# Seven node steps in a row between the first loads and the first tile of the message stage

## The chip, the cores and the metric

The kernel runs on one core of a Trainium2 chip. The metric is the device time of one execution in microseconds (us), the median over several executions. Engines are named PE (TensorE, matmuls and transposes), DVE (VectorE), ACT (ScalarE), POOL (GpSimd) and SP (SyncE, which here only issues DMAs and waits).

## What is computed

A graph network with two message-passing layers over 50000 nodes of 256 features and 12500 edges sorted by destination. Each layer adds its result to the node rows and normalises them:

```python
x = _layernorm(x + _L0_gnn_ref(x, edge_index, L0_gnn_W, L0_gnn_attn, L0_gnn_W_out), axis=-1)
x = _layernorm(x + _L1_gnn_ref(x, edge_attr_64, edge_index, ...), axis=-1)
```

The first layer is attention over the edges (scores, softmax over the edges of one destination, weighted sum, product with W_out). The second layer has the same shape with queries, keys and values, adds edge attributes, and mixes its result with a skip product under a sigmoid gate:

```python
x_r = m @ Wskip.T + bskip
beta = jax.nn.sigmoid(jnp.concatenate([out, x_r, out - x_r], axis=-1) @ Wbeta.T)
out = beta * x_r + (1.0 - beta) * out
return out @ W_m2n.T
```

A node that no edge ends in has out = 0 in both layers, so its row is a normalisation, one product with a folded matrix, a gated add and a second normalisation. Rows that edges end in are computed apart, by edge, and scattered over the first result at the end.

## The kernel before

There are two kinds of work. **Node steps** (class Nodes) take all 50000 rows, 256 rows (two tiles of 128) at a time, as if no edge ended in any: 196 steps, 205 with the drain of their pipeline. **Edge tiles** are 100 tiles of 125 edges that pass through stages in turn: score, first softmax (soft1), gather, message, second softmax (soft2), output. A softmax stage is one serial chain over all tiles. Edge tiles of one stage write rows to DRAM which the next stage reads.

One hand-written list, the plan, holds (part, step) entries. Each engine walks the same plan from first to last and issues what that part does on it at that step, so that on each engine the order of instructions is the plan's, and an instruction that waits holds up all that stands behind it on its engine. The function blend spreads two lists evenly through each other. NODE_SHARE says how many node entries are blended into the start (74), soft1 (10), gather (66), message (45) and soft2 (10).

A node entry s works on several steps of the pipeline at once, by `live(s, lag, total)`. On SP it issues the load of step s + 2 (L635), and then the store of step s - 9 (L651). X has 12 slots, and the load must wait for the slot's earlier store to have landed. That is the store of step s - 10, which the node entry just ahead has issued:

```python
n = s + self.AHEAD
at_least(sp, self.moved[n % U], 32 * (n // U))
load(n)
```

On DVE a node entry takes the statistics of row block s (L763, waits for its load), the gated add of s - 5 (L770), the aggregate (L778) and, at every second entry, the normalisation of s - 2 (L784; at the others one small operation L757 for ACT, which then normalises). On PE it issues four transposes (L734) and four matmuls with the folded matrix (L744). On POOL it computes 1/sqrt of the variances with L666 and L671; DVE and ACT of the next entry wait for it. ACT copies, squares and scales; the scaled rows are what the store waits for.

A gather entry's PE part is two transposes (L1210) and two matmuls (L1217) after a scan on DVE (L1243). Each tile's row block is loaded from rows, added to, and stored again (L1186). A message entry t, from -6 to 102, loads on SP the row block of tile t + 5 (L1337) and for every second tile a line of picks (L1340), and issues on POOL the indirect gather of source rows for tile t + 5 (L1307). Entry -6 clears a buffer (DVE L1426) and loads edge attributes (L1347). At entry -5 three things stand in front of the first loads: POOL waits until all stores of the gather stage have landed, then gathers 100 tail rows (L1304); SP waits for those, writes them to DRAM (L1334), and waits for that write. DVE takes statistics of tile t + 3 (L1440, L1453), compares picks of tile t + 2 (L1459) and normalises tile t + 1 (L1467). From entry 0 on PE transposes tile t (L1367, L1369), and one entry later it computes keys, values and queries (L1382, L1383, L1387). POOL's L1315 and L1318 compute 1/sqrt for two tiles together.

Of the kernel before, what the change touches and what calls it, by code (L numbers as in the profile page):

```python
# [71 lines left out]
def blend(lists):  # L72

    spread = [((2 * k + 1) / (2 * len(x)), n, entry) for n, x in enumerate(lists) for k, entry in enumerate(x)]
    return [(n, entry) for _, n, entry in sorted(spread, key=lambda e: e[:2])]
# [1588 lines left out]
def main_pass(nc, c, io, out):  # L1664

    with ExitStack() as ctx:
# [21 lines left out]
        output = Output(nc, c, ctx, out, masks, nodes, message, soft2)  # L1688
        parts = (nodes, score, finder, soft1, gather, message, soft2, output, made, masks, positions)
        plan = order_of(parts, NODE_SHARE)  # L1690

        with nc.Block() as block:
# [28 lines left out]
                    emits[n](s)  # L1721


NODE_SHARE = (74, 10, 66, 45, 10)
NODE_NORMED = ["A" if 74 <= s < 84 or s >= 186 else "AD"[s % 2] if s >= 84 else "D" for s in range(NSTEPS)]
NODE_SCALED = ["AD"[s % 2] if s < 66 else "A" for s in range(NSTEPS)]

# [1 line left out]
def order_of(parts, share):  # L1729


    nodes, score, finder, soft1, gather, message, soft2, output, made, masks, positions = range(11)
    entries = [[(n, s) for s in range(p.FIRST, p.LAST)] for n, p in enumerate(parts)]
    at = share[0]
    plan = start_of(entries[score], entries[finder], entries[nodes][0:at], entries[made], entries[masks], entries[positions])
    for count, group in zip(share[1:], ((soft1,), (gather,), (message,), (soft2,))):
        lists = [entries[nodes][at:at + count]] + [entries[n] for n in group]
        at += count
        plan += [entry for _, entry in blend(lists)]
    assert at == len(entries[nodes])  # L1740
    return plan + entries[output]
# [8 lines left out]
def start_of(score, finder, nodes, made, masks, positions):  # L1750


    before = {}
    for at, part in ((MADE_AT, made), (MASKS_AT, masks), (POSITIONS_AT, positions)):
        for t, entry in zip(at, part):
            before.setdefault(t, []).append(entry)
    steps = [e for e in score]
    plan = []
    for at, tiles in ((Score.FIRST, NODES_FROM), (NODES_FROM, FINDER_FROM), (FINDER_FROM, Score.LAST)):
        part = steps[at - Score.FIRST:tiles - Score.FIRST]  # L1760
        share = round(len(nodes) * len(part) / (Score.LAST - NODES_FROM)) if tiles < Score.LAST else len(nodes)
        now = [] if at < NODES_FROM else nodes[:share]
        nodes = nodes[len(now):]
        lists = [now, part] + ([finder] if at == FINDER_FROM else [])
        for n, entry in blend(lists):
            if n == 1:
                plan += before.pop(entry[1], [])
            plan.append(entry)
    assert not nodes and not before
    return plan  # L1770
# [92 lines left out]
```

How the kernel before makes its waits and increments, by code:

```python
def at_least(eng, sem, value):  # L50
    if value > 0:
        eng.wait_ge(sem, value)
# [118 lines left out]
        @block.sync  # L172
# [16 lines left out]
                sp.dma_start(w.w_n2m, io["L1_gnn_W_n2m"]).then_inc(c.ldd, 16)  # L189
                for k in range(2):
                    sp.dma_start(w.w_edge[:, k, :], io["L1_gnn_W_edge"]).then_inc(c.ldd, 16)
                for k in range(2):
                    sp.dma_start(c.wo[:, k, :], io["L0_gnn_W_out"][k * P:(k + 1) * P, :]).then_inc(c.ldd, 16)
                sp.wait_ge(dve_done, 4)
                sp.dma_start(w.previ[1:TILES, :], rows[0:TILES - 1, EDGES - 1:EDGES]).then_inc(c.edge_loads, 16)
                sp.dma_start(w.nexti[0:TILES - 1, :], rows[1:TILES, 0:1]).then_inc(c.edge_loads, 16)
# [3 lines left out]
        @block.scalar  # L200
        def _(act):
            with nc.allow_non_contiguous_dma(reason="one bias column"):
                for out, name in ((w.bq_xr[:, 0:DM], "bq"), (w.bq_xr[:, DM:2 * DM], "bskip"), (w.b_kv[:, 0:DM], "bk"), (w.b_kv[:, DM:2 * DM], "bv")):
                    act.dma_start(out, io["L1_gnn_" + name].rearrange("(a d) -> a d", a=1).to_broadcast([P, DM])).then_inc(c.ldd, 16)
                act.dma_start(w.bs_cols[:, 0:1], io["L1_gnn_bskip"].rearrange("(d a) -> d a", a=1)).then_inc(c.ldd, 16)
            act.wait_ge(turned, 1)
            for k, out in enumerate((c.src_col, c.dst_col)):
                act.activation(out[:, :], c.psum[:, 0, k * 256:k * 256 + TILES], ACT.Copy).then_inc(turned, 1)
```

## Time and profile before

| | us |
|---|---|
| median of 3 executions | 1315.22 |
| lowest and highest | 1313.17, 1316.82 |
| profiled execution, whole | 1313.72 |
| its span, first to last instruction | 1311.9 |
| PE busy | 1170.9 (89%) |
| DVE busy | 1050.2 (80%) |
| ACT busy | 841.8 (64%) |
| POOL busy | 836.8 (64%) |

In the trace the first softmax lies at about 390 to 440 us, the gather stage at 440 to 727, the message stage at 727 to 1075. Busy time is the time in which an engine executes; a row of a timeline gives start and duration of merged instructions, how many, and in square brackets how long the engine was idle before them and what ended the wait. A row of SP gives the issue of a DMA, not its transfer. LDWEIGHTS (PEld) runs beside PE's matmuls.

### The profile page before, as it was taken

How to read it: one execution, taken by the hardware profiler on the slowest of the kernel's cores; microseconds unless marked ns; L12 is line 12 of the kernel's file. 1: busy time of each engine (PE TensorE's matmuls, PEld its weight loads, DVE VectorE, ACT ScalarE, POOL GpSimd, SP SyncE). 2: the span in 40 equal slices, each digit the busy share in tenths (PEclk: the TensorE clock that was granted, in tenths of full speed). 3: DMA queues.
4: the chain of work that ended last, by engine and by line, in shares of the span. 5: the costliest groups of instructions: out<-in, count | busy, mean ns of one | idle time of the engine just before them, and what ended most of it. 6: DMA issues, size and time to landing. Idle time of an engine off the chain costs nothing. (4 is left out here: it accounts for less than half of the span.)

```text
span 1311.9 us, 28292 instructions
## 1 busy us (share of the span) xinstructions
PE 1170.9 (89%) x6986; PEld 1022.4 (78%) x6986; DVE 1050.2 (80%) x3776; ACT 841.8 (64%) x2783; POOL 836.8 (64%) x1044
## 2 busy tenths in 40 slices
PE   3999999999996789989999599999999993999991
PEld 3888998989985577778777498999999982788880
DVE  3667777777779798899888599999999977788881
ACT  1566666666667756656666466666666675799992
POOL 4888888888853445445453566667767732377775
PEclk9999999999998999999999799999999997999996
DMA  5768988888863478878787777777767732556641
GB/s 155 237 207 268 280 258 265 257 282 268 260 223 121 145 230 237 244 239 258 225 251 213 230 218 216 213 215 233 218 213 218 218 105 86 163 184 191 191 157 56
DMA packets 208938, 277.05 MB, mean 211 GB/s; under 512 B 40060, under 2 KB 140563, under 8 KB 208777
## 3 DMA queue, kind: packets, MB, share of 16 engines
q1 hardware_dynamic: 188793, 224.13, 55.5%
q0 software_dynamic: 19264, 50.85, 13.4%
q8 instruction: 60, 0.98, 0.3%
q14 instruction: 101, 0.83, 0.2%
q10 hardware_dynamic: 720, 0.26, 0.1%
HBM read 159.73 MB, written 117.12 MB: 211 GB/s over the span
## 5 line engine op out<-in xcount | busy, mean ns | idle before, releaser
L744 PE MATMUL banks<-m_ext,node_XT 128*128 128x257 f32 x1568 | 377.1, 383 | 0.0
L744 PEld LDWEIGHTS banks<-m_ext,node_XT 128*128 128x128 f32 x1568 | 286.0, 192 | 32.8
L671 POOL TENSOR_TENSOR node_r<-node_vv,half 128x4 f32<-128x4 f32 (+1 forms) x202 | 211.9, 1049 | 17.2 <-POOL node_vv L666 0.5
L702 ACT ACTIVATE node_XT<-banks 128x512 f32<-128x512 f32 x196 | 117.1, 597 | 153.1 <-PE banks L734 150.1
L770 DVE SCALAR_TENSOR_TENSOR node_X<-banks,node_be,node_X 128x256 f32<-128x256 f32 x392 | 169.2, 473 | 56.3 <-ACT node_be L696 56.0
L666 POOL TENSOR_SCALAR node_vv<-node_mv 128x4 f32<-128x4 f32 (+1 forms) x202 | 54.9, 272 | 200.6 <-DVE node_mv L778 180.5
L763 DVE BATCH_NORM_STATS2 node_st<-node_X 128x6 f32<-128x256 f32 x392 | 145.7, 413 | 20.6 <-DMA node_X<-in_x 19.4
L709 ACT ACTIVATE node_sq<-node_X 128x256 f32<-128x256 f32 x392 | 157.5, 406 | 0.0
L683 ACT ACTIVATE node_X<-node_X,node_r 128x256 f32<-128x256 f32 x326 | 146.0, 496 | 16.3 <-POOL node_r L671 16.2
L734 PE MATMUL banks<-ident,node_X 128*128 128x128 f32 x784 | 122.4, 279 | 31.9 <-DVE node_X L784 16.8
L824 POOL DMA_INDIRECT ring<-in_x,src_col x100 | 110.7, 1107 | 36.4 <-POOLq L171 13.7
L734 PEld LDWEIGHTS banks<-ident,node_X 128*128 128x128 f32 x784 | 95.6, 149 | 44.9 <-issue 19.7
L1307 POOL DMA_INDIRECT ring<-rows,src_pos x100 | 107.3, 1073 | 22.8 <-issue 20.3
L784 DVE TENSOR_SCALAR node_X<-node_X,node_mv,node_r 128x256 f32<-128x256 f32 x250 | 91.1, 406 | 34.0 <-POOL node_r L671 34.0
L824 POOL DMA_INDIRECT ring<-in_x,dst_col x100 | 98.2, 982 | 31.5 <-issue 29.0
L857 PE MATMUL banks<-wh,ST 128*128 128x260 f32 x400 | 105.3, 386 | 1.1
L870 ACT ACTIVATE ST<-banks 128x512 f32<-128x512 f32 x100 | 59.3, 593 | 73.0 <-PE banks L847 71.4
L1538 POOL DMA_INDIRECT out<-store,last_col x90 | 89.1, 990 | 26.3 <-issue 20.0
L1382 PE MATMUL banks<-w_kv,ST 128*128 128x256 f32 x400 | 104.9, 385 | 0.3 <-DVE store L1430 0.3
L1580 PE MATMUL banks<-m_ext,AT 128*128 128x257 f32 x400 | 104.3, 383 | 0.0
L1217 PE MATMUL banks<-wo,AT 128*128 128x256 f32 x400 | 103.0, 380 | 0.2 <-DVE ring L1234 0.2
L1243 DVE TENSOR_TENSOR_SCAN AT<-MB,AT,banks 128x128 f32<-128x128 f32 x198 | 83.9, 465 | 18.7 <-PE banks L1210 13.4
(267 smaller groups left out, 2674.6 us busy)
## 6 DMA issues: line engine op xcount, KB each, us to landing
node_X<-in_x SPq DMA_DIRECT2D x196, 256.0 KB, 3.8
out<-node_X SPq DMA_DIRECT2D x196, 256.0 KB, 3.3
ring<-rows SPq DMA_DIRECT2D x210, 128.0 KB, 4.2
rows<-ring SPq DMA_DIRECT2D x100, 256.0 KB, 4.4
rows<-ring SPq DMA_DIRECT2D x200, 128.0 KB, 3.5
MB<-keeps SPq DMA_DIRECT2D x40, 320.0 KB, 5.2
store<-rows SPq DMA_DIRECT2D x90, 128.0 KB, 4.1
MB<-picks SPq DMA_DIRECT2D x50, 128.0 KB, 3.9
```

What stands on the lines that cost most here:

```text
L671: pool.tensor_tensor(r[:, s % 4, NT * lo:NT * hi], v, self.c.half[:, NT * lo:NT * hi], ALU.pow).then_inc(self.roots, 1)
L683: last = eng.activation(row, row, ACT.Identity, scale=rz)
L702: act.activation(self.XT[:, n % 2, :], c.psum[:, 4, 0:NT * D], ACT.Copy, bias=1.0).then_inc(self.xt_ready, 1)
L709: last = act.activation(self.sq[:, k, :], X[:, n % U, k, :], ACT.Square, scale=1.0 / D ** 0.5, accum_out=self.mv[:, s % 4, 1, k, 1:2])
L734: last = pe.transpose(ps[:, 4, k * D + h * P:k * D + (h + 1) * P], self.X[:, n % U, k, h * P:(h + 1) * P], c.ident[:, :])
L744: last = pe.matmul(ps[:, NT * o + k, 0:D + 1], self.XT[:, o, k * D + h * P:k * D + (h + 1) * P], c.m_ext[:, h, :], start=(h == 0), stop=(h ...
L763: last = dve.bn_stats(st[:, s % 2, k, :], X[:, s % U, k, :])
L770: last = dve.scalar_tensor_tensor(out=X[:, n % U, k, :], in0=ps[:, b + k, 0:D], scalar=self.be[:, n % 4, k:k + 1], in1=X[:, n % U, k, :], ...
L824: pool.indirect_dma_start(out=c.ring[:, n % R, side, :], out_offset=None, in_=self.x, in_offset=bass.IndirectOffsetOnAxis(ap=col[:, n:n + ...
L857: pe.matmul(ps[:, 6, 0:HP], c.ST[:, o, h * P:(h + 1) * P], c.wh[:, h, :], start=(h == 0), stop=(h == 1))
L1307: pool.indirect_dma_start(out=c.ring[:, n % R, 1, :], out_offset=None, in_=c.rows, in_offset=bass.IndirectOffsetOnAxis(ap=c.src_pos[:, n:n ...
L1382: pe.matmul(ps[:, 6, 0:2 * DM], c.ST[:, o, h * P:(h + 1) * P], c.w_kv[:, h, :], start=(h == 0), stop=(h == 1))
```

## The change

Two node entries move from the gather stage to the message stage (NODE_SHARE 66 and 45 become 64 and 47). The message stage's first three entries (-6, -5, -4), which issue the loads and gathers of tiles 0 and 1, come first without nodes between them. Then seven node entries follow in a row, and only then the other 106 message entries blended with the other 40 node entries. The rest of the program is unchanged.

```diff
-NODE_SHARE = (74, 10, 66, 45, 10)
+NODE_SHARE = (74, 10, 64, 47, 10)
+NODES_AT_MESSAGES = 7
+MESSAGES_AFTER = 3
...
     for count, group in zip(share[1:], ((soft1,), (gather,), (message,), (soft2,))):
-        lists = [entries[nodes][at:at + count]] + [entries[n] for n in group]
+        now, others = entries[nodes][at:at + count], [entries[n] for n in group]
         at += count
+        if group == (message,):
+            plan += others[0][:MESSAGES_AFTER] + now[:NODES_AT_MESSAGES]
+            now, others = now[NODES_AT_MESSAGES:], [others[0][MESSAGES_AFTER:]]
+        lists = [now] + others
         plan += [entry for _, entry in blend(lists)]
```

On SP at the start of the message stage, before the change (L1347 is entry -6, each pair L635 and L651 a node entry, L1334 the write of the tail rows, L1337 a tile's row block):

```order
L1347 DMA MSG<-in_edge_attr 125x4x64
L635 DMA node_X<-in_x 128x512
L651 DMA out<-node_X 128x512
L1334 DMA rows<-AT 100x256
L1337 DMA ring<-rows 128x256
L1340 DMA MB<-picks 128x256
L1337 DMA ring<-rows 128x256 x2
L1340 DMA MB<-picks 128x256
L635 DMA node_X<-in_x 128x512
L651 DMA out<-node_X 128x512
L1337 DMA ring<-rows 128x256
L1347 DMA MSG<-in_edge_attr 125x4x64
```

and with the change:

```order
L1347 DMA MSG<-in_edge_attr 125x4x64
L1334 DMA rows<-AT 100x256
L1337 DMA ring<-rows 128x256
L1340 DMA MB<-picks 128x256
L1337 DMA ring<-rows 128x256
L635 DMA node_X<-in_x 128x512
L651 DMA out<-node_X 128x512
L635 DMA node_X<-in_x 128x512
L651 DMA out<-node_X 128x512
...
L635 DMA node_X<-in_x 128x512
L651 DMA out<-node_X 128x512
L1337 DMA ring<-rows 128x256
```

The load of tile 2 was the third L1337, directly behind those of tiles 0 and 1; now seven node entries (the first two and the last are shown, four are like them) stand between.

On DVE from the buffer's clearing at entry -6 on, before the change (L763 to L784 are node entries, the first L1440 is entry -3):

```order
L1426 MEMSET MSG 128x512
L757 SCALAR_TENSOR_TENSOR node_nb<-node_mv,node_r 128x2
L763 BN_STATS node_st<-node_X 128x6 x2
L770 SCALAR_TENSOR_TENSOR node_X<-banks,node_be,node_X 128x256 x2
L778 BN_AGGR node_mv<-node_st 128x2 x2
L1440 BN_STATS message_st<-ring 128x6 x2
L1453 BN_AGGR message_mv<-message_st 128x2 x2
L763 BN_STATS node_st<-node_X 128x6 x2
L770 SCALAR_TENSOR_TENSOR node_X<-banks,node_be,node_X 128x256 x2
L778 BN_AGGR node_mv<-node_st 128x2 x2
L784 TENSOR_SCALAR node_X<-node_X,node_mv,node_r 128x256 x2
L1440 BN_STATS message_st<-ring 128x6 x2
```

and with the change, where the rows left out are five more node entries:

```order
L1426 MEMSET MSG 128x512
L757 SCALAR_TENSOR_TENSOR node_nb<-node_mv,node_r 128x2
L763 BN_STATS node_st<-node_X 128x6 x2
L770 SCALAR_TENSOR_TENSOR node_X<-banks,node_be,node_X 128x256 x2
L778 BN_AGGR node_mv<-node_st 128x2 x2
...
L763 BN_STATS node_st<-node_X 128x6 x2
L770 SCALAR_TENSOR_TENSOR node_X<-banks,node_be,node_X 128x256 x2
L778 BN_AGGR node_mv<-node_st 128x2 x2
L1440 BN_STATS message_st<-ring 128x6 x2
L1453 BN_AGGR message_mv<-message_st 128x2 x2
L763 BN_STATS node_st<-node_X 128x6 x2
```

One node entry stood ahead of the first statistics of a message tile (L1440), and now seven do. Up to tile 0 on PE there were three node entries, and now eight; up to tile 2 there were four, and now nine. In the gather stage each run of tiles between two node entries has one or two tiles: 23 runs of one and 42 of two before the change, 19 and 44 with it.

## Rows read from the trace of the kernel before

**Rows 1.** Busy time in stretches: us, then PE, PEld, DVE, ACT, POOL, clock, DMA share

```profile
460.00:700.00 240.00, 220.87 (x1183) 183.12 (x1182) 210.91 (x679) 147.50 (x487) 122.56 (x198) 1.00 0.81 241
760.00:1060.00 300.00, 296.90 (x1974) 272.43 (x1973) 281.32 (x1203) 188.96 (x553) 209.18 (x258) 1.00 0.73 217
```

**Rows 2.** Timeline of PE in the gather stage: start, duration, line, operation

```profile
457.32 0.60 PE L734 MATMUL banks<-ident,node_X 128*128 128x128 f32 x4
...
566.67 0.60 PE L734 MATMUL banks<-ident,node_X 128*128 128x128 f32 x4
...
569.93 0.60 PE L734 MATMUL banks<-ident,node_X 128*128 128x128 f32 x4
...
574.63 0.60 PE L734 MATMUL banks<-ident,node_X 128*128 128x128 f32 x4
...
714.94 0.60 PE L734 MATMUL banks<-ident,node_X 128*128 128x128 f32 x4
```

**Rows 3.** Timeline of PE in the middle of the message stage

```profile
863.11 0.60 PE L734 MATMUL banks<-ident,node_X 128*128 128x128 f32 x4
...
865.29 0.38 PE L1367 MATMUL banks<-ident,ring 128*128 128x128 f32 x2
```

**Rows 4.** Timeline of SP's DMA queue around the stage boundary

```profile
712.54 0.33 SPq L635 DMA_DIRECT2D node_X<-in_x  x1
...
726.82 0.33 SPq L635 DMA_DIRECT2D node_X<-in_x  x1
727.25 0.38 SPq L651 DMA_DIRECT2D out<-node_X  x1
...
732.46 0.30 SPq L1334 DMA_DIRECT2D rows<-AT  x1
735.86 0.32 SPq L1337 DMA_DIRECT2D ring<-rows  x1
...
736.71 0.90 SPq L1337 DMA_DIRECT2D ring<-rows  x2
```

**Rows 5.** Timeline of DVE around the stage boundary

```profile
715.38 0.75 DVE L763 BATCH_NORM_STATS2 node_st<-node_X 128x6 f32<-128x256 f32 x2 [0.45 <-DMA node_X<-in_x]
...
738.29 0.75 DVE L1440 BATCH_NORM_STATS2 message_st<-ring 128x6 f32<-128x256 f32 x2 [10.42 <-DMA ring<-rows]
...
739.24 0.72 DVE L763 BATCH_NORM_STATS2 node_st<-node_X 128x6 f32<-128x256 f32 x2
...
741.43 0.74 DVE L1440 BATCH_NORM_STATS2 message_st<-ring 128x6 f32<-128x256 f32 x2
...
749.32 0.75 DVE L1440 BATCH_NORM_STATS2 message_st<-ring 128x6 f32<-128x256 f32 x2 [0.90 <-DMA ring<-rows,src_pos]
...
750.44 0.82 DVE L1467 TENSOR_SCALAR ring<-ring,message_mv,message_r 128x256 f32<-128x256 f32 x2
```

**Rows 6.** Timeline of POOL around the stage boundary

```profile
728.22 1.15 POOL L1304 DMA_INDIRECT AT<-rows,tail_pos  x1 [2.43 <-issue]
...
744.10 1.20 POOL L1307 DMA_INDIRECT ring<-rows,src_pos  x1 [0.20 <-issue]
```

**Rows 7.** Timeline of PE around the first message tiles

```profile
745.37 0.38 PE L1367 MATMUL banks<-ident,ring 128*128 128x128 f32 x2
...
754.43 0.38 PE L1367 MATMUL banks<-ident,ring 128*128 128x128 f32 x2
```

**Rows 8.** Timeline of SP's DMA queue in the first softmax

```profile
397.07 0.38 SPq L651 DMA_DIRECT2D out<-node_X  x1
400.42 0.33 SPq L635 DMA_DIRECT2D node_X<-in_x  x1
...
406.34 0.34 SPq L651 DMA_DIRECT2D out<-node_X  x1
408.37 0.33 SPq L635 DMA_DIRECT2D node_X<-in_x  x1
...
429.79 0.33 SPq L635 DMA_DIRECT2D node_X<-in_x  x1
```

## Prediction

> **What bounds the kernel now.** I read the busy time by stretches first. In the middle of the message stage PE is busy 296.9 of 300 us at full clock [rows 1], so there a node step costs what it occupies PE: from its first transpose at 863.11 to the next tile's at 865.29, 2.18 us [rows 3]. In the gather stage PE is busy 92% and DVE 88% [rows 1]; neither is full, and a node step's price must come from the spacing of rows [rows 2]. Between the stages lies a gap, and I read it engine by engine on the timelines. POOL issues the tail gather at 728.22 [rows 6]; SP writes the tail rows at 732.46, waits for them, and issues the first row block at 735.86 [rows 4]; DVE idles 10.42 us until that lands, at 738.29 [rows 5]; PE transposes tile 0 at 745.37 and tile 2 at 754.43 [rows 7]. From there on PE hardly pauses. The change puts work into this gap, so the question is what the row of seven costs there and what it saves elsewhere.
>
> **What it saves in the gather stage.** Two node steps leave. From 457.32 to 714.94 there are 58 intervals between node steps on PE [rows 2]: 20 with one tile in them, 3.27 us each in the mean (569.93 less 566.67 is one of them), and 38 with two tiles, 5.06 us in the mean (most are 4.70, as 574.63 less 569.93). The stage goes from 23 short and 42 long intervals to 19 and 44, so it saves 4 x 3.27 - 2 x 5.06 = 3.0 us, or 4 x 3.27 - 2 x 4.70 = 3.7 with the usual long one. I take 3.3. The other bound is that steps, not tiles, set the pace: 257.6 us for 58 steps is 4.44 us each, and two save 8.9.
>
> **What it saves among the message tiles.** The milestone is tile 2 on PE, since PE works without a break from there. Before it stood four node steps of 45, so 41 came after; now nine of 47, so 38. Three steps at 2.18 us are 6.5 us. Against this being less stands nothing: PE is 99% busy there [rows 1]. If DVE (94% busy) took over, the price would be its step, 741.43 less 739.24, again 2.2 us [rows 5].
>
> **What the row of seven costs.** A node step's load waits on SP until the store that the step just ahead issued has landed. In a run of node steps this is a chain of its own: store, landing, load, next store. The trace shows it where the gather stage drains: four steps from 712.54 to 726.82, 3.57 us each [rows 4], and DVE waits for their loads, as at 715.38, 2.84 us after the issue at 712.54 [rows 4, 5]. PE would need 2.18, DVE 2.2. So SP's DMAs set the pace of a row of node steps, and nothing hides them.
>
> Nor can the row start inside the wait. On SP the seven stand behind the write of the tail rows and the wait for it, so the first of them issues its load at about 737.2, after the second row block (736.71 and half of its 0.90 us [rows 4]). POOL meets the first of the seven only after the tail gather at 728.22 and two tile gathers. From what was loaded already, DVE and PE can do two steps in the gap; the third needs the load of 737.2.
>
> From there, in the clock of the trace before: the seventh node load at 737.2 + 6 x 3.57 = 758.6, its store at 759.0 (0.43 later, as 727.25 after 726.82 [rows 4]), the row block of tile 2 at 759.5. Its landing and the start on DVE took 2.43 us (735.86 to 738.29 [rows 4, 5]), so DVE has it at 761.9. This load is late because it moved behind the seven; tiles 0 and 1 have lain ready since 740. DVE's entry for tile 2 also normalises tile 0, behind the statistics of tile 2. Such an entry takes 749.32 to 750.44 and 0.82 more, 1.9 us [rows 5]. Tile 0 is on PE at 763.8, 18.4 us later than at 745.37 [rows 7].
>
> The next entries: SP's eighth node step waits for the store of 759.0 until 762.2 (3.14 us, which is 3.57 less the 0.43), so the row block of tile 3 goes out at 763.0 and is there at 765.5. DVE works on it until 767.4, does a node step (2.2) until 769.6, and the entry of tile 4 (1.9), behind which tile 2 is normalised at 771.5. POOL's gather for tile 4 must wait for the inverse roots of tiles 0 and 1, about 762.5, and takes 5.2 us (744.10 to 749.32 [rows 5, 6]), which is 767.9 and not late. Tile 2 is on PE at about 771.4 instead of 754.43: 17.0 us later.
>
> **The sum.** 17.0 - 6.5 - 3.3 = +7.2 us. Against the profiled execution's 1313.72 that is 1320.9; the median of the runs shown is 1.5 higher, 1315.22, so I predict 1322.4 us, 0.55% slower. Put another way, five more steps go into a stretch that grows by 17.0 us, 3.4 us a step, and are paid back at 2.0.
>
> **A rule against the row.** The node store of 256 KB lands 3.1 to 3.4 us after its issue when a load of the same size stands right before it: 3.35 from 397.07 to 400.42, in a stretch where next to nothing else moves [rows 8]. The store issued alone at 406.34 lets the next load go at 408.37, after 2.03 us [rows 8]. In the row of seven every store follows a load by 0.43 us, so I keep 3.57 for the step. The Trainium skill (DMA: Bandwidth & Descriptors, section on the anatomy of one DMA) puts a transfer at a fixed 2.0 us, mostly waiting for the write's receipt, and its bytes at 436 GB/s; an estimate by that page is 2.6 us for a store, 3.0 a step, and a sum of about +3.9. The row with the load ahead speaks against it, the lone store for something shorter still.
>
> **The rivals.**
> - Stores land quickly because little else is moving, at 2.03 us as the lone one [rows 8]. The step is then 2.46, six intervals save 6.7, and the sum is +0.5: 1315.7. For it speaks the lone store, against it the 3.35 us in the same quiet stretch. The same page's section on latency says that lighter load on HBM shortens the fixed part, which is this rival. Chance 0.09.
> - Node steps set the gather stage's pace, 4.44 us each [rows 2]: 17.0 - 6.5 - 8.9 = +1.6, 1316.8. Against it: intervals differ by their tiles, 3.27 and 5.06. Chance 0.14.
> - The other side: the wait covers the row. If the node steps run while DVE waits its 10.42 us [rows 5], five more of them at 2.18 are 10.9, so tile 2 is late by only 0.5 us, and 0.5 - 6.5 - 3.3 = -9.3: 1305.9. It decides on SP at the wait for the tail rows: tile 2 must be late by less than 9.8 us for any gain, by less than 5.9 for one to be seen. Against it stands the order on SP and POOL, where the seven are behind that wait. Chance 0.10.
> - ACT's scaled rows come late for the stores, as in the first softmax, where five steps from 408.37 to 429.79 took 4.28 each [rows 8]. Six intervals add 4.3: 1326.7. There the softmax held up DVE and ACT; the row of seven has nothing between, but PE's clock may drop after the idle time and lengthen the chain a little. Chance 0.13.
> - That the change doesn't do what it says is ruled out by the order of the two programs.
>
> **Numbers.** The forecast keeps 0.54. About 0.3% is what a measurement of this kernel can tell from no change, 3.9 us here. Slower by more: most of 0.54 and all of 0.13, less a small part for a forecast too high by half, 0.63. Within 0.3%: the two rivals at +0.5 and +1.6 and that part, 0.26. Faster: 0.11. The range of 1314.5 to 1328.0 takes in all but the third rival and some remainder: below it reaches under +0.5, above to +4.3 on the forecast and a little more for first tiles at a lower clock.
>
> **What the changed profile would show.** On SP seven pairs of node load and store 3.5 to 3.7 us apart, with waits for the node store, and L1337 for tile 2 some 22 us after those of tiles 0 and 1. DVE waiting before L763 in the row rather than before the first L1440. Tile 0 (first L1367) 17 to 19 us later, seen from the tail gather L1304. The tail gather itself some 3.3 us earlier than 728.22, and from tile 2 to the end of the message stage 6.5 us less. I am wrong if the pairs stand 2.5 us apart, if the gather stage shrinks by 8 us, or if some pairs come before L1334.

## The result

The changed kernel takes 1318.99 us (median of 8, 1315.41 to 1321.31) against 1314.04 us for the kernel before on the same chip (median of 8, 1309.12 to 1316.82): a ratio of 1.0035, 95% interval 1.0021 to 1.0049, or 4.6 us slower by the ratio and 4.95 by the medians. The forecast was 7.2 us slower, and 1322.4 us. Its profiled execution has a span of 1315.8 us, 3.9 more than before.

Three points in time cut the trace into parts: POOL's first weighted row of the gather stage (L1175), the tail gather (L1304), and tile 2 of the message stage on PE (third L1367). The first is read from the view of one line, here of the kernel before and then of the changed one; the pair of times is that of the first and the last such instruction.

```profile
L1175 POOL TENSOR_TENSOR MSG<-store,weights x100: 608/614/617, 440.1 to 701.1; 128x256 f32<-128x256 f32 x100
```

```profile
L1175 POOL TENSOR_TENSOR MSG<-store,weights x100: 607/612/616, 438.1 to 691.7; 128x256 f32<-128x256 f32 x100
```

The tail gather on POOL's timeline of the changed kernel, which answers to the first line of [rows 6]:

```profile
717.76 1.15 POOL L1304 DMA_INDIRECT AT<-rows,tail_pos  x1 [5.83 <-issue]
```

So the gather stage took 728.2 - 440.1 = 288.1 us before and 717.8 - 438.1 = 279.7 with the change. On PE's timeline, as in [rows 7], the first three message tiles, and two of the node steps ahead of them (L744, eight matmuls, 1.90 us at full clock):

```profile
730.75 2.86 PE L744 MATMUL banks<-m_ext,node_XT 128*128 128x257 f32 x8 [2.77 <-DVE node_X L770]
...
736.00 3.14 PE L744 MATMUL banks<-m_ext,node_XT 128*128 128x257 f32 x8
...
754.83 0.69 PE L1367 MATMUL banks<-ident,ring 128*128 128x128 f32 x2 [6.95 <-DVE ring L1467]
...
759.74 0.38 PE L1367 MATMUL banks<-ident,ring 128*128 128x128 f32 x2
...
762.42 0.44 PE L1367 MATMUL banks<-ident,ring 128*128 128x128 f32 x2 [0.32 <-DVE ring L1467]
```

Tile 2 comes at 762.42, 44.7 us after the tail gather; before it was 26.2 us (754.43 less 728.22). Between them lies the row of seven. SP's queue there, as in [rows 4]:

```profile
721.28 0.28 SPq L1334 DMA_DIRECT2D rows<-AT  x1
...
724.59 0.42 SPq L1337 DMA_DIRECT2D ring<-rows  x1
725.05 0.43 SPq L635 DMA_DIRECT2D node_X<-in_x  x1
725.58 0.38 SPq L651 DMA_DIRECT2D out<-node_X  x1
729.75 0.33 SPq L635 DMA_DIRECT2D node_X<-in_x  x1
...
733.37 0.33 SPq L635 DMA_DIRECT2D node_X<-in_x  x1
...
744.55 0.33 SPq L635 DMA_DIRECT2D node_X<-in_x  x1
...
748.46 0.33 SPq L635 DMA_DIRECT2D node_X<-in_x  x1
...
749.35 0.43 SPq L1337 DMA_DIRECT2D ring<-rows  x1
```

The first node load of the row goes at 725.05, behind the tail rows and the row block of tile 1, and the seventh at 748.46: six intervals of 3.90 us in the mean. Each load but the first waits for the landing of the store just ahead, the first time from 725.58 to 729.75; by the view of SP's waits these six waits hold 18.2 us. The row block of tile 2 goes out at 749.35, 24.8 us after that of tile 1. DVE waits for node rows in the row, as it waited for the tile's row block before [rows 5]:

```profile
722.88 0.73 DVE L784 TENSOR_SCALAR node_X<-node_X,node_mv,node_r 128x256 f32<-128x256 f32 x2 [2.33 <-POOL node_r L671]
...
729.07 0.75 DVE L763 BATCH_NORM_STATS2 node_st<-node_X 128x6 f32<-128x256 f32 x2 [4.69 <-DMA node_X<-in_x]
...
739.76 0.75 DVE L763 BATCH_NORM_STATS2 node_st<-node_X 128x6 f32<-128x256 f32 x2 [1.95 <-DMA node_X<-in_x]
...
745.01 0.72 DVE L1440 BATCH_NORM_STATS2 message_st<-ring 128x6 f32<-128x256 f32 x2
...
752.92 0.76 DVE L1440 BATCH_NORM_STATS2 message_st<-ring 128x6 f32<-128x256 f32 x2 [1.66 <-issue]
```

At 722.88 it ends the second step of the row, which needs no further load; from 729.07 on it waits for the loads. Tile 0's statistics (L1440, 745.01) follow the row directly, and tile 2's at 752.92 stand between them and the normalisation of tile 0.

The lengths of the parts, for all kernels that ran. "Row" is the change's row of node entries; "last" is the last L1367. The first two and the next two lines are the same kernel twice.

| kernel (gather/message shares) | gather stage | tail gather to tile 2 | tile 2 to last | last to end | median us |
|---|---|---|---|---|---|
| before (66/45) | 288.1 | 26.2 | 316.1 | 241.3 | 1314.04 |
| before again | 288.4 | 24.8 | 316.9 | 241.9 | (one: 1314.36) |
| changed (64/47, row) | 279.7 | 44.7 | 311.7 | 241.7 | 1318.99 |
| changed again | 276.7 | 44.9 | 311.5 | 242.6 | (one: 1316.21) |
| shares alone (64/47) | 281.1 | 25.5 | 317.4 | 243.2 | 1304.87 |
| row alone (66/45) | 284.5 | 45.5 | 306.7 | 241.7 | 1323.34 |
| two in a row (64/47) | 280.2 | 27.3 | 320.3 | 242.4 | 1309.85 |
| row behind six (64/47) | 278.6 | 38.3 | 312.7 | 241.9 | 1314.01 |
| shares 58/53 | 263.4 | 25.1 | 329.4 | 244.3 | 1298.04 |
| before, 13 slots | 271.9 | 25.2 | 316.7 | 243.0 | 1297.45 |
| changed, 13 slots | 267.0 | 38.6 | 310.5 | 242.9 | 1298.67 |
| shares 58/53, 13 slots | 257.6 | 23.6 | 329.4 | 243.7 | 1295.11 |
| row behind six, 13 slots | 265.8 | 37.8 | 312.5 | 241.6 | 1299.81 |
| row behind six, 58/53, 13 slots | 255.7 | 40.4 | 322.4 | 244.8 | 1302.38 |

The medians come from four sessions, in which the kernel before stood at 1312.3 to 1314.0; ratios below are each against the runs of before in its own session. One profiled execution may lie 2 to 5 us from its kernel's median (1319.46 against 1323.34 for the row alone, 1303.28 against 1298.04 for the shares 58/53), so a part's length is good to some 2 us, and the gather stage's to 4: up to there the three kernels with 66 entries run the same program but for the last node entry, and theirs took 284.5 to 288.4 us, and the five with 64 took 276.7 to 281.1. With 13 slots the mark between the first two columns moves too. In the kernel before with 13 slots the tail gather comes 6.3 us after the last store of the gather stage (SP 704.51 to POOL 710.82), held up on POOL by the one node entry ahead of it; with the row that entry stands behind it, and it comes 3.0 us after (701.92 to 704.96). So 3.3 us of what the gather stage loses and the stretch gains between those two lines is only the mark. With 12 slots it comes 4.2 and 4.1 us after in the two kernels.

### The profile page after: what moved, and what is told of

It is laid out like the page before. It is cut to its first block and busy times, and to the rows that moved or that the text cites. A ratio compares the mean times of both kernels' runs of the same rounds, so it can differ in the third digit from the quotient of the medians.

```text
span 1315.8 us, 28292 instructions
## 1 busy us (share of the span) xinstructions
PE 1177.1 (89%) x6986; PEld 1025.7 (78%) x6986; DVE 1050.6 (80%) x3776; ACT 841.7 (64%) x2783; POOL 835.8 (64%) x1044
## 5 line engine op out<-in xcount | busy, mean ns | idle before, releaser
L744 PE MATMUL banks<-m_ext,node_XT 128*128 128x257 f32 x1568 | 381.1, 386 | 2.8 <-DVE node_X L770 2.8
L744 PEld LDWEIGHTS banks<-m_ext,node_XT 128*128 128x128 f32 x1568 | 288.6, 194 | 36.7 <-issue 3.1
L671 POOL TENSOR_TENSOR node_r<-node_vv,half 128x4 f32<-128x4 f32 (+1 forms) x202 | 211.4, 1047 | 17.3 <-ACT node_X L683 0.4
L702 ACT ACTIVATE node_XT<-banks 128x512 f32<-128x512 f32 x196 | 117.0, 597 | 143.0 <-PE banks L734 140.1
L763 DVE BATCH_NORM_STATS2 node_st<-node_X 128x6 f32<-128x256 f32 x392 | 145.9, 414 | 26.9 <-DMA node_X<-in_x 25.9
L683 ACT ACTIVATE node_X<-node_X,node_r 128x256 f32<-128x256 f32 x326 | 146.1, 496 | 21.9 <-POOL node_r L671 21.9
L734 PE MATMUL banks<-ident,node_X 128*128 128x128 f32 x784 | 123.7, 281 | 27.9 <-DVE node_X L784 13.1
L784 DVE TENSOR_SCALAR node_X<-node_X,node_mv,node_r 128x256 f32<-128x256 f32 x250 | 91.5, 408 | 42.8 <-POOL node_r L671 42.8
L870 ACT ACTIVATE ST<-banks 128x512 f32<-128x512 f32 x100 | 59.3, 593 | 70.8 <-PE banks L847 68.6
L1409 ACT ACTIVATE ST<-banks 128x512 f32<-128x512 f32 x100 | 59.3, 593 | 67.5 <-PE banks L1369 67.5
```

Of the source, the lines that this page charges most:

```text
L671: pool.tensor_tensor(r[:, s % 4, NT * lo:NT * hi], v, self.c.half[:, NT * lo:NT * hi], ALU.pow).then_inc(self.roots, 1)
L683: last = eng.activation(row, row, ACT.Identity, scale=rz)
L702: act.activation(self.XT[:, n % 2, :], c.psum[:, 4, 0:NT * D], ACT.Copy, bias=1.0).then_inc(self.xt_ready, 1)
L734: last = pe.transpose(ps[:, 4, k * D + h * P:k * D + (h + 1) * P], self.X[:, n % U, k, h * P:(h + 1) * P], c.ident[:, :])
L744: last = pe.matmul(ps[:, NT * o + k, 0:D + 1], self.XT[:, o, k * D + h * P:k * D + (h + 1) * P], c.m_ext[:, h, :], start=(h == 0), stop=(h ...
L763: last = dve.bn_stats(st[:, s % 2, k, :], X[:, s % U, k, :])
```

## The experiments

**The change in halves.** First the shares without the row.

```diff
-NODE_SHARE = (74, 10, 66, 45, 10)
+NODE_SHARE = (74, 10, 64, 47, 10)
```

> Only the shares change: two node entries go from the gather stage to the message stage (64 and 47), blended evenly in both, no row of seven. Theory A (my prediction's terms): the gather stage saves 3.3 us by the count of its short and long intervals, two more steps among message tiles cost 2 x 2.2, so +1.1 us. Theory B (from the changed kernel's trace, whose gather stage, first weighted row to tail gather, was 279.7 us instead of 288.2): fewer steps there save 8.5 us by themselves, so -4.1 us, and the gather stage of this run is also near 280.

Measured: 1304.87 us, ratio 0.9944 (0.9928 to 0.9960), 7.4 us faster. My terms fall; the gather stage of this run is 281.1 us. The two steps are worth 7 us there by this trace against that of before, and theory B holds, with more gained than its 4.1 us.

Then the row without the shares, that is the changed kernel with

```diff
-NODE_SHARE = (74, 10, 64, 47, 10)
+NODE_SHARE = (74, 10, 66, 45, 10)
```

> Only the row of seven: shares as before (66 and 45), the first three message entries, seven node entries, then the rest. Theory A: tail gather to tile 2 on PE grows by 17 to 18.5 us as in the changed kernel, and five steps fewer after tile 2 give 10.9 back: +6.1 to +7.6 us. Theory B (node steps are worth less among tiles, 1.8 us): +8.5 to +9.5 us. Theory C (the stretch between the stages costs less when it isn't preceded by a shorter gather stage): below +4.

Measured: 1323.34 us, ratio 1.0090 (1.0073 to 1.0107), 11.8 us slower. The stretch is 45.5 us, 19 to 21 longer than before, and tile 2 to last gives back 9.4 to 10.2 for five steps. That is nearest to theory B, but its time is above the bounds of all three, since the stretch grew by more than any of them had. This trace's gather stage, 284.5 us, is 3.7 shorter than the mean of the two of before with the same shares; it is the execution that lies 3.9 us below its kernel's median. The halves add up: -7.4 + 11.8 = +4.4 us, against +4.6 for both together.

**The wait for the store just issued.** With 13 slots instead of 12, the load of step s + 2 waits for the store of step s - 11, which the node entry before the last has issued. To make room, the squares that nothing reads are stored as bf16; the ACT instruction that writes them takes 408 ns in the median instead of 407.

```diff
-    U = 12
+    U = 13
...
-        self.sq = sb("sq", [P, NT, D])
+        self.sq = sb("sq", [P, NT, D], mybir.dt.bfloat16)
```

The kernel before, so changed:

> The kernel before with 13 instead of 12 slots for node rows (room for it by storing the unused squares as bf16): a node's load then waits for the store two steps back and not for the one just issued. Theory A (the store's landing paces node steps only where they stand in a row): the five steps where the gather stage drains take some 2.5 us instead of 3.57, 4 to 6 us are saved there and in the first softmax, and the gather stage's inner intervals stay at 3.3 and 4.7 to 5.1. Theory B (the landing also paces the inner gather stage): the long intervals lose their excess over 4.7 and the stage shrinks by more than 10 us.

Measured: 1297.45 us, ratio 0.9882 (0.9864 to 0.9900), 15.5 us faster. What SP waited for between 460 and 690 us (total, times, longest), in the kernel before and then with 13 slots:

```profile
SPq L635 <- DMA out<-node_X: 74.0, 47, 4.5
...
SPq L1186 <- DVE ring L1234: 5.6, 15, 0.8
```

```profile
SPq L1186 <- DVE ring L1234: 40.8, 33, 2.3
SPq L53 <- ACT node_X L683: 37.9, 32, 2.6
```

The wait of the node load for a landing store, 74.0 us over 47 times, is gone; SP now waits for what the engines have ready, scaled node rows from ACT (L683) and edge rows from DVE (L1234). The bf16 squares weren't run with 12 slots, so that they do nothing for the time rests on ACT's unchanged duration. The gather stage shrinks from 288.1 to 271.9 us, so theory B holds: the long intervals between node steps on PE (two tiles in them, 5.06 us in the mean before [rows 2]) are 4.72 us in the mean now, 38 of them in either trace. The landing of stores paced part of the inner gather stage too. This is the fact that my gather term had wrong.

The changed kernel with 13 slots:

> The changed kernel with 13 slots. Theory A (the wait of a load for the store just issued sets the pace of the row of seven): the seven node loads stand 2.2 to 2.7 us apart instead of 3.9 in the mean, the stretch from the tail gather to tile 2 shrinks by 7 to 9 us, and the change costs nothing any more against the kernel before with 13 slots (-4 to 0 us). Rival (the engines' own chain or PE's lower clock after the idle time sets the pace): the loads stay 3.3 us or more apart and the change still costs 3 us or more.

Measured: 1298.67 us, above the kernel before with 13 slots by 1.2 us by the medians and by 2.8 by the ratios (0.9903 and 0.9882 to the same runs, whose intervals overlap), where the change cost 4.6 with 12. So it costs less, but the forecast of -4 to 0 isn't shown. SP's node loads in the row:

```profile
712.23 0.43 SPq L635 DMA_DIRECT2D node_X<-in_x  x1
...
713.18 0.43 SPq L635 DMA_DIRECT2D node_X<-in_x  x1
...
717.21 0.33 SPq L635 DMA_DIRECT2D node_X<-in_x  x1
...
725.73 0.43 SPq L635 DMA_DIRECT2D node_X<-in_x  x1
727.50 0.34 SPq L651 DMA_DIRECT2D out<-node_X  x1
```

From 712.23 to 725.73 there are six intervals of 2.25 us in the mean, where they were 3.90, so the chain of store, landing and load is shown to have set the pace. The waits for landing stores aren't all gone: four of them hold 6.5 us in this row, against six and 18.2. The stretch shrinks from 44.7 to 38.6 us, by 6.1 where 7 to 9 were expected, and not to the 25.2 of the kernel without a row. On PE the node steps now follow each other like this:

```profile
721.47 0.60 PE L734 MATMUL banks<-ident,node_X 128*128 128x128 f32 x4
...
724.58 0.63 PE L734 MATMUL banks<-ident,node_X 128*128 128x128 f32 x4 [0.77 <-issue]
...
727.08 0.66 PE L734 MATMUL banks<-ident,node_X 128*128 128x128 f32 x4
...
730.24 0.63 PE L734 MATMUL banks<-ident,node_X 128*128 128x128 f32 x4 [0.77 <-issue]
```

That is 8.77 us for three steps, 2.92 us each, where PE needs 2.18 [rows 3]: with no tiles between them, PE waits in each or in every second step until rows have gone through the other engines. The fullest of them is ACT, busy for 8.02 of these 8.77 us, with PE at 7.11 and DVE at 6.50.

**Fewer in the row.** Two instead of seven, which is as many as are already loaded:

```diff
-NODES_AT_MESSAGES = 7
+NODES_AT_MESSAGES = 2
```

> The changed kernel with two node entries in a row instead of seven (shares 64 and 47 as changed). Two steps' rows are loaded before SP waits for the tail rows. Theory A (only steps beyond the two loaded ones cost the interval of 3.6 to 3.9 us): tail gather to tile 2 on PE takes 26 to 28 us instead of 44.7, and the time stands within 3 us of the kernel with only the shares changed (-7.4 against the kernel before). Rival (the first tiles suffer from anything that stands before them, by the row blocks loaded late): the stretch is 32 us or more, the time 5 us or more over the shares alone.

Measured: 1309.85 us, ratio 0.9977 (0.9961 to 0.9993), 3.0 us faster than before but over 4 slower than the shares alone by the ratios, which is between the two theories' bounds. The stretch is 27.3 us, as theory A has it; 1.8 us of the difference are there, and some 3 lie between tile 2 and the last tile (320.3 against 317.4). Some 2 of these are one node step more: 42 stand between those two tiles on PE, and 41 with the shares alone, which has one more behind the last tile (243.2 against 242.4 us to the end). From two to seven in the row the stretch grows by 17.3 us, 3.46 us a step.

**The row behind six message entries.** Five row blocks are then issued ahead of the row, and tile 0 is normalised.

```diff
-MESSAGES_AFTER = 3
+MESSAGES_AFTER = 6
```

> The row of seven moves behind six message entries instead of three: row blocks and gathers of tiles 0 to 4 are issued and tile 0 is normalised before the seven; tile 0 on PE comes right behind them. Theory A (of the 19 us, 6 or 7 intervals are the node loads' chain and some 8 us are the row block of tile 2 that comes late and the tile pipeline started anew): tail gather to tile 2 takes 36 to 38 us instead of 44.7, with 8 node steps before tile 2 instead of 9, and the time is 5 to 8 us below the changed kernel's, near that of before. Rival (the chain of node loads is all of it): no better than 2 us below the changed kernel.

Measured: 1314.01 us, ratio 1.0007 (0.9991 to 1.0024): level with before, some 3.7 us below the changed kernel by the ratios. PE's timeline:

```profile
719.87 0.66 PE L1358 MATMUL banks<-ident,MSG 128*128 128x128 f32 x2 [6.31 <-DMA MSG<-in_edge_attr]
...
731.25 1.09 PE L734 MATMUL banks<-ident,node_X 128*128 128x128 f32 x4 [6.43 <-issue]
...
749.20 0.38 PE L1367 MATMUL banks<-ident,ring 128*128 128x128 f32 x2
...
752.34 0.38 PE L1367 MATMUL banks<-ident,ring 128*128 128x128 f32 x2
...
754.87 0.44 PE L1367 MATMUL banks<-ident,ring 128*128 128x128 f32 x2 [0.17 <-DVE ring L1467]
```

Tile 0 follows the row at once and tile 1 after 3.1 us, where it was 4.9, and the stretch is 38.3 us, just above the expected 36 to 38. The time gained, 3.7 us, is less than the 5 to 8 of theory A and more than the 2 of its rival. One reason stands in the first two lines: PE first waits 6.31 us for the edge attributes, with node steps ready behind, and then 6.43 us more, since DVE takes the tiles' statistics before the row. The gap that the first steps of the row had filled is empty again.

**Both together.** The row behind six entries and 13 slots:

> The changed kernel's row of seven behind six message entries, with 13 slots: both suspected costs are taken away, the chain of node loads behind stores and the late row block of tile 2. Theory A (these two are the whole excess of the stretch): tail gather to tile 2 takes 31 to 33 us, with four more node steps before tile 2 than in the kernel before with 13 slots (25.2 us), so under 2 us a step; the time is 1294 to 1297, level with or below the 1297.5 of the kernel before with 13 slots. Rival (something else in the row costs, such as PE's lower clock or the engines' own chain): the stretch stays at 36 us or more and the time at 1298 or above.

Measured: 1299.81 us, ratio 0.9899 (0.9882 to 0.9917). Theory A falls, and its rival holds: the stretch is 37.8 us. SP's queue, PE's timeline and ACT's in the row:

```profile
729.26 0.70 SPq L635 DMA_DIRECT2D node_X<-in_x  x1
732.38 0.34 SPq L651 DMA_DIRECT2D out<-node_X  x1
732.76 0.94 SPq L635 DMA_DIRECT2D node_X<-in_x  x1
734.53 0.34 SPq L651 DMA_DIRECT2D out<-node_X  x1
```

```profile
710.25 0.66 PE L1358 MATMUL banks<-ident,MSG 128*128 128x128 f32 x2 [4.67 <-DMA MSG<-in_edge_attr]
...
719.24 1.09 PE L734 MATMUL banks<-ident,node_X 128*128 128x128 f32 x4 [4.06 <-issue]
...
722.85 0.60 PE L734 MATMUL banks<-ident,node_X 128*128 128x128 f32 x4
...
734.10 0.66 PE L734 MATMUL banks<-ident,node_X 128*128 128x128 f32 x4
```

```profile
726.62 0.60 ACT L702 ACTIVATE node_XT<-banks 128x512 f32<-128x512 f32 x1
...
729.14 0.60 ACT L702 ACTIVATE node_XT<-banks 128x512 f32<-128x512 f32 x1 [0.28 <-PE banks L734]
...
732.27 0.60 ACT L702 ACTIVATE node_XT<-banks 128x512 f32<-128x512 f32 x1
```

SP's loads and stores alternate and hardly a load waits for a store any more (0.3 us in all); the stores wait for scaled rows instead (17.0 us by the view of waits, nine times from 700 to 760 us, for ACT). PE does the last four steps from 722.85 to 734.10, 2.81 us each. And PE idles in the gap as before. So beyond the two costs there is a third, and the traces name the engine: two steps take ACT 5.65 us, from the copy (L702) at 726.62 to that at 732.27, and the 0.28 before 729.14 are all it idles in them. ACT is busy for 10.51 of the 11.25 us of the four steps, PE for 9.47 and DVE for 7.33. A node step occupies ACT for some 2.7 us, since every step's rows are scaled there and every second step's also normalised; that is more than PE's 2.18 and DVE's 2.2, the two that my prediction compared. No run moved work off ACT, so that a row would then go faster is not shown.

PE's clock isn't the reason in these steps: the granted clock is 1.00 from 722.85 to 734.10 here, and 1.00 in the three steps of the changed kernel with 13 slots shown above. In the whole stretch it was 0.81 and 0.85 in the two traces of the changed kernel and 0.74 and 0.79 in those of before, so some steps run at half the clock (L744 in 2.86 and 3.14 us above), but the row didn't lower it. That the gap can be filled only by what stands ahead of DVE's first tile is my reading of the order of the work; no run put the row there.

**How the gather stage prices a node step.** Eight entries moved instead of two, no row:

```diff
-NODE_SHARE = (74, 10, 66, 45, 10)
+NODE_SHARE = (74, 10, 58, 53, 10)
```

> The kernel before with 58 node entries blended into the gather stage and 53 into the message stage. My prediction's terms (a gather stage of intervals of 3.27 and 5.06 us: 16 short ones fewer, 8 long ones more; 2.18 us a step in the message stage): gather -11.8, message +17.4, so +5.6 us. What the shares alone showed (gather about 3 us a step, message 1.5 to 1.8): gather -24, message +13, so -9 to -13 us. If the gain of the shares alone was a matter of where the two steps stood, it doesn't grow: -7 to 0.

Measured: 1298.04 us, ratio 0.9890 (0.9866 to 0.9915), 14.4 us faster, a little beyond the 9 to 13 that the shares alone led me to expect. The gather stage is 24.7 us shorter, 3.1 us a step, and tile 2 to last 13.3 longer, 1.7 a step. The forecast from my prediction's terms, +5.6 us, has even the sign wrong. The same with 13 slots:

> The same shares, 58 and 53, with 13 slots, so that a load doesn't wait for the store just issued. Theory A (part of a node step's price in the gather stage is the landing of stores, which 13 slots take away, and the rest PE's 3.26 and 4.72 us intervals): the gather stage is 13 to 16 us shorter than with 66 steps and 13 slots, the message stage 12 to 15 longer, so the time is within 3 us of the 1297.5 of 13 slots alone. Rival (a step costs 3 us in the gather stage whatever the slots): 8 us or more below it.

Measured: 1295.11 us, ratio 0.9875 (0.9852 to 0.9898), the fastest of all and 1.25% faster than before. Against 13 slots alone it is 2.3 us less by the medians and 0.9 by the ratios. The gather stage gives 14.3 us, 1.8 a step, and the message stage takes 12.7. With the landing out of the way a step costs about the same in either stage, and moving steps brings next to nothing. That is theory A.

**A try for a faster one.** 58/53, 13 slots and the row behind six entries:

> The same with shares 58 and 53, as the candidate for the fastest. If the terms add up: 13 slots and 58/53 measured 1295.1, and the row behind six entries is worth 0 to -3 more: 1292 to 1295. If the row only moves work about: 1295 to 1297.

Measured: 1302.38 us, ratio 0.9917 (0.9898 to 0.9935): 5.5 us slower than without the row by the ratios and 7.3 by the medians, so neither forecast held. The stretch is 40.4 us against 23.6, and tile 2 to last gives back only 7.0.

**The same kernels again.** For the spread of the parts:

> The kernel before, unchanged, for a second trace: how far the lengths of its stages move between executions. If the gather stage's 288.1 us was typical, this one is within 1 us of it, and two steps fewer saved 7 to 8 us there. If that execution was a long one, this is near the 284.5 us of the kernel with the row alone, and two steps saved about 4 to 5 us. Tail gather to tile 2 within 1 us of 26.2 in either case.

> The changed kernel, unchanged, for a second trace. Gather stage within 1.5 us of 279.7, tail gather to tile 2 within 1.5 us of 44.6, tile 2 to the last tile within 1.5 us of 311.7.

The gather stage of before is 288.4 us again; that of the changed kernel is 276.7, 3.0 below the first, so that forecast missed. Two steps fewer saved 8.4 to 11.7 us by these four traces and 7.0 by the shares alone; the mean over all three traces with 66 entries is 287.0 us and over all five with 64 it is 279.3, which makes 7.8. The stretch of before, 24.8, is 1.4 below the first where 1 was allowed; that of the changed kernel (44.9) and tile 2 to last (316.9 and 311.5) repeat.

## Why the prediction was right, and where it wasn't

The sign and the place were right: the row of seven costs more in the stretch between the stages than its steps cost elsewhere. The sum of 17.0 - 6.5 - 3.3 should have read, from the two traces of each kernel, 19.3 - 4.9 - 10.1 = +4.3, against the measured +4.6. Each term was off, and that the forecast came near is in part luck: the gather stage gave 6.8 us more than I had, and the other two terms, 2.3 and 1.6 us off the other way, took more than half of it back. Nor does +4.3 bear out the +4.6 to a few tenths, since the whole spans of the same four traces differ by only 2.8 us (1315.8 and 1314.4 against 1311.9 and 1312.6): the first softmax ended 1.9 us earlier in the two of the changed kernel, and 0.5 more went by behind the last tile.

- **The stretch, 17.0.** Measured 19.3 (44.7 and 44.9 against 26.2 and 24.8). The chain was as described: seven pairs behind the tail rows, loads waiting for the store just issued, the row block of tile 2 behind them, tile 0 held by tile 2's statistics. The mis-sized step is the interval: I took 3.57 us from the drain of the gather stage, and it was 3.90, which over six is 2.0 us. The first interval was 4.70, the fifth 4.17, the other four 3.44 to 3.91. Two smaller errors nearly cancel: the first load of the row went out 7.3 us after the tail gather (717.76 to 725.05) where I had 9.0, and from the row block of tile 2 to tile 2 on PE it took 13.1 and 13.5 us where I had 11.9. By the same chain tile 0 came 19.7 us later than before, seen from the tail gather, where I had said 17 to 19.
- **The gather stage, 3.3.** Here the working failed, and my own sign of being wrong, a gather stage 8 us shorter, came true (8.4 in the first traces). I counted short and long intervals and held the mean of the long ones fixed. But the long ones' excess over 4.7 us was itself the wait for landing stores, and with fewer steps it fell: 4.91 us in the mean for 41 long ones in the changed kernel, 5.06 for 38 before. In the traces of the two halves the mean was 4.97 (66 entries) and 4.95 (64), so how far it falls with two steps fewer is known only roughly. The rival's 8.9 for two steps is nearer to what the traces show (7.8 in the mean), but not for its reason: that would be 4.44 us a step whatever the slots. The runs with 13 slots show the cause, since without that wait the long intervals are 4.72, the stage is 16 us shorter, and eight steps moved out of it save 1.8 us each instead of 3.1, near the 1.65 of my count.
- **The message tiles, 6.5.** Measured 4.4 to 5.4 for three steps, 9.8 for five in the row alone, 13.3 for eight in the other direction: 1.6 to 2.0 us a step and not the 2.18 for which a step occupies PE. A likely reason, worked out from the intervals and not tested, is that fewer steps leave longer runs of tiles, and these carry waits of their own: an interval with two tiles took 6.84 us and one with three 9.36 (means of before), which is 2.52 for the third tile, more than the 2.34 from one tile to the next without a wait (867.59 to 869.93 on PE before). By these means three steps fewer turn nine intervals of two tiles into six of three and save an estimated 5.4 us, 1.8 a step.

Of the rivals, the one on the gather stage was near in its term and wrong in its result, since the other two terms moved against it. The quick store (2.03 us) didn't appear in the row: every store there followed a load by half a microsecond and landed late. The estimate by the Trainium skill's fit (DMA: Bandwidth & Descriptors, the anatomy of one DMA), 3.0 us a step, was short of the 3.90 that the trace shows. That section gives its fit for DMAs that GpSimd issues, and the stores here are issued by SP, so the fit isn't tested by them. The sum of +3.9 by it is near the result only because the gather stage's term was off. The rival in which the wait covers the row would need node loads ahead of the tail rows, and none was. That ACT's scaled rows hold up the stores doesn't hold with 12 slots, where all six loads wait for a landing store, but it is what comes next with 13. The prediction should have had ACT's 2.7 us a step beside PE's 2.18 and DVE's 2.2; with 12 slots it changed nothing, as the 3.90 lie above it.

What stays open is why the first softmax ended earlier in every other kernel than in the two traces of before (L1175 at 437.7 to 439.3 against 440.1 and 440.6), with the same program up to there wherever there are 12 slots, and what makes the gather stage of one program differ by 3 to 4 us between executions.

## What to carry to other kernels

A ring of buffers where a load must wait for the store issued by the step just ahead has a pace of its own, here 3.6 to 3.9 us, whatever the engines could do. Look for that wait in the DMA queue's own view: in the gather stage DVE waited for node rows for only 11.4 of 230 us (460 to 690), and yet one more buffer took away 1.2% of the whole time. Moving eight steps out of the stage took away 1.1% without that buffer and next to nothing more with it. Work put behind the wait that causes a gap doesn't fill the gap, it makes it longer, here by 19 us for five more steps; that work fed ahead of the wait on every queue would fill it is the conclusion, but no run here tried it. When one engine's price of a step is compared, compare all of them: ACT's was the highest here. Where a change does two things, run them apart: here one half was worth 7.4 us and the other lost 11.8.

## What was unexpected of the hardware

A store of 256 KB that follows a load of 256 KB on SP's queue by 0.43 to 0.53 us let the next load go 3.0 to 4.2 us after its issue (725.58 to 729.75 is the longest in the row), against 2.03 for one issued alone [rows 8], in a stretch where DMA moved 184 GB/s (718 to 763 us), against 241 and 217 in the stages around it (the last column of [rows 1]). I had expected the quiet stretch to be the quick one. The four stores of the first softmax that were issued 1.9 us or more behind a load (406.34, 419.44, 423.43 and 427.51 before) let the next load go after 2.03 to 2.28 us. So the short time goes with the distance to the load ahead and not with the traffic as a whole; why was not tested.
